# Beside-copies cut into four, and attention work moved between the convolutions, in a four-layer convolution chain

## The reference

```python
# layer 0
q2 = _l2n(q2 / (jnp.sum(q2, axis=2, keepdims=True) + 1e-07), axis=2)
k2 = _l2n(k2 / (jnp.sum(k2, axis=2, keepdims=True) + 1e-07), axis=1)
kv = jnp.einsum('bnc,bnd->bcd', k2, v)
t2 = jnp.einsum('bnc,bcd->bnd', q2, kv) / math.sqrt(N)
attn = (v + t2) @ w_ln + b_ln
...
y = jax.nn.leaky_relu(_conv(y, w1, 'VALID') + b1, 0.2)
y = jax.nn.leaky_relu(_conv(y, w2, 'SAME') + b2, 0.2)
y = _conv(y, w3, 'VALID') + b3
return y + shortcut
# layers 1 and 3
y = lax.conv_general_dilated(jax.nn.relu(x), dw_kernel, ..., feature_group_count=C)
y = lax.conv_general_dilated(y + dw_bias, pw_kernel, ...) + pw_bias
```

## Time and profile before

| what | us |
|---|---|
| median of 3 runs (1218.30 to 1224.15) | 1218.42 |
| the profiled execution, its own time | 1220.06 |
| its span on the core | 1218.2 |
| TensorE busy with matmuls (90% of the span) | 1092.2 |
| VectorE busy (70%) | 855.1 |
| ScalarE busy (39%) | 473.6 |
| a full iteration, from one pair convolution's start to the next one's (392.33 to 529.44) | 137.1 |

### The profile page before, as it was taken

One profiled execution on the slowest core, in us unless ns is written; L12 is line 12 of the kernel. 1 busy time (PEld: TensorE's weight loads), 2 busy tenths in 40 slices (PEclk: granted clock), 3 DMA queues, 4 the chain that ended last, 5 costly groups with the idle time before them and its releaser, 6 DMA issues.

```text
span 1218.2 us, 14814 instructions
## 1 busy us (share of the span) xinstructions
PE 1092.2 (90%) x5000; PEld 704.7 (58%) x5000; DVE 855.1 (70%) x1182; ACT 473.6 (39%) x812; POOL 90.4 (7%) x72
## 2 busy tenths in 40 slices
PE   4698779979998999989998999989998999987956
PEld 3465656647664666647664666647664666645414
DVE  6732379955799369965799369965799369962940
ACT  3311534235522644245522644245522644243321
POOL 0300021000200021000200021000200021000000
PEclk9899879989999999999999999999999999998987
DMA  4033513089405943089405943089405930089035
GB/s 61 14 57 46 71 23 39 12 98 120 65 0 71 104 77 39 0 110 117 65 0 72 106 75 39 2 112 113 65 0 76 107 69 1 6 112 125 12 41 73
DMA packets 213503, 72.97 MB, mean 60 GB/s; under 512 B 206464, under 2 KB 207333, under 8 KB 213477
## 3 DMA queue, kind: packets, MB, share of 16 engines
q1 hardware_dynamic: 213476, 72.63, 45.4%
HBM read 10.49 MB, written 6.29 MB: 14 GB/s over the span
## 4 chain that ended last, share of the span: by engine, by line
PE 46%; DVE 23%; issue 16%; DMA 5%; SPq 5%; ACT 4%; DVEq 0%; POOL 0%; ACTq 0%; POOLq 0%
PE bank L1119 12%; DVE dwa L647 8%; DVE dwb L647 5%; PE bank L1095 5%; DMA y_parts<-a_parts 5%; PE bank L1077 4%; PE bank L1122 4%; PE bank L1121 4%; PE bank L1032 3%; SPq L866 3%; PE bank L1187 2%; SPq L862 2%; PE bank L1134 2%; PE bank L1069 2%; PE bank L1042 2%
## 5 line engine op out<-in xcount | busy, mean ns | idle before, releaser
L647 DVE SCALAR_TENSOR_TENSOR dwa<-h1a,dyn,dwa 128x1024 f32<-128x1024 f32 x240 | 293.4, 1273 | 0.0
L1095 PE MATMUL bank<-y_parts,w_h 96*96 96x512 f32 x1152 | 292.9, 403 | 0.0
L1095 PEld LDWEIGHTS bank<-y_parts,w_h 96*96 96x96 f32 x1152 | 184.3, 162 | 104.5 <-issue 21.0
L1119 PE MATMUL bank<-a_parts,wt_h 128*112 128x512 f32 x384 | 122.4, 429 | 60.5 <-DMA y_parts<-a_parts 52.8
L647 DVE SCALAR_TENSOR_TENSOR dwb<-h1b,dyn,dwb 128x1024 f32<-128x1024 f32 x128 | 154.8, 1274 | 0.0
L1095 PE MATMUL bank<-y_parts,w_l 96*96 96x512 f32 x576 | 148.0, 401 | 0.0
L1119 PEld LDWEIGHTS bank<-a_parts,wt_h 128*112 128x112 f32 x384 | 67.1, 185 | 91.2 <-DMA y_parts<-a_parts 34.3
L1095 PEld LDWEIGHTS bank<-y_parts,w_l 96*96 96x96 f32 x576 | 93.4, 162 | 44.3
L967 POOL TENSOR_TENSOR y_parts<-y,y_parts 96x512 fp32r<-96x512 f32 x56 | 67.0, 1199 | 191.9 <-DVE y L686 191.8
L1350 ACT ACTIVATE y<-bank,b2s 96x512 f32<-96x512 f32 x32 | 21.9, 684 | 146.0 <-PE bank L1095 146.0
L961 POOL TENSOR_TENSOR tok<-tok,u 128x1536 f32<-128x1536 f32 x8 | 22.4, 2794 | 727.7 <-DVE u L584 727.7
(11 more groups left out here) (236 smaller groups left out, 1570.6 us busy)
## 6 DMA issues: line engine op xcount, KB each, us to landing
y_parts<-a_parts SPq DMA_DIRECT2D x32, 396.0 KB, 6.1
y_parts<-a_parts SPq DMA_DIRECT2D x64, 192.0 KB, 6.7
tok<-in_x_dram SPq DMA_DIRECT2D x48, 192.0 KB, 4.8
a_parts<-a_parts SPq DMA_DIRECT2D x64, 132.0 KB, 3.8
x_even<-y_parts SPq DMA_DIRECT2D x16, 384.0 KB, 8.0
x_odd<-y_parts SPq DMA_DIRECT2D x16, 384.0 KB, 8.1
out_dram<-dwb SPq DMA_DIRECT2D x32, 192.0 KB, 3.6
y_parts<-a_parts SPq DMA_DIRECT2D x32, 132.0 KB, 4.3
```

Source lines behind the costliest of these rows:

```text
L647: nc.vector.scalar_tensor_tensor(out=dst, in0=tap_input(n, t), scalar=weight, in1=dst, op0=ALU.mult, op1=ALU.add).then_inc(tap_step, 1)
L1095: last = nc.tensor.matmul(bank[0:C2, :], wgt[:, t, :], src[:, rows, cols], start=t + n == 0, stop=t == TAPS - 1 and n == 2)
L1119: nc.tensor.matmul(bank[0:P2, :], wgt[layer][:, kw, :], own[:, rows, kw:kw + W], start=n + kw == 0, stop=False)
```

## The change

Four things are changed together.

- **Copies by quarters.** `copy_beside` takes a quarter (8 pairs of rows) instead of a half, so there are 32 copies for each layer and image instead of 16, each of half the bytes. Quarter m waits for chunks 0 to m+1 of the high and low parts, and for layer 1 to `conv2` chunk m+1, for layer 3 to `l1` chunk m. `pair_conv` waits at every chunk for its own quarter.
- **Scores earlier.** TensorE does l1 0, transposes 0 and 1, l1 1, transposes 2 and 3, scores, and then project 2 and 3, then l1 2 and 3.
- **Attention between layer 3's chunks.** After l1 come l3 0, routing, sums, l3 1, tokens 0, gather, l3 2, tokens 1, attention weights, l3 3, tokens 2, halo, tokens 3, conv1.
- **ScalarE and VectorE follow.** ScalarE squares the first four scores before it takes l1 1 out, the other four after it, then finishes units 4 and 5, and then does project's chunks 2 and 3 and the fourth powers. VectorE begins the norms before it writes x2's low parts 2 and 3; `sums_out` is split, and its first part (`sums_apart`) stands ahead of `mix_weights`.

```diff
@@ -245,7 +245,7 @@
             sem(n) for n in ("xq_ready", "y1_slope", "y1_max", "y1h_ready", "y1l_ready", "y1l_last"))
         y2_slope, y2_ready, v_ready, ah1_ready, al1_ready = (sem(n) for n in ("y2_slope", "y2_ready", "v_ready", "ah1_ready", "al1_ready"))
 
-        b_copied = {n: (sem(f"b{n}_first_copied"), sem(f"b{n}_rest_copied")) for n in (L1, L3)}
+        b_copied = {n: [sem(f"b{n}_copied{m}") for m in range(PCHUNKS)] for n in (L1, L3)}
         x2_ready, x2h_ready, x2l_ready, x2_copied = (sem(n) for n in ("x2_ready", "x2h_ready", "x2l_ready", "x2_copied"))
         mean_ready, rwz_ready, rw_ready = (sem(n) for n in ("mean_ready", "rwz_ready", "rw_ready"))
         tap1_ready = sem("tap1_ready")
@@ -600,13 +600,16 @@
                 nc.vector.tensor_tensor(q, q, columns(r[:, :, :], 0, [[1, 2 * RUN], [0, C]]), ALU.mult).then_inc(q_scaled, 1)
                 attn2_chain.end()
 
-            def sums_out(image):
+            def sums_apart(image):
 
                 bank = ring_a.bank(A_G)
                 dve.wait_ge(g_done, 2 * image + 2)
                 for at in (0, ODD_AT):
                     nc.vector.tensor_copy(gs[at:at + C, :], bank[at:at + C, 0:SUMS]).then_inc(gs_ready, 1)
-                both_parities = bank[0:SUMS, 128:128 + C]
+
+            def sums_out(image):
+
+                both_parities = ring_a.bank(A_G)[0:SUMS, 128:128 + C]
                 dve.wait_ge(gt_done, image + 1)
                 nc.vector.tensor_copy(gt[:, :], both_parities).then_inc(gt_ready, 1)
                 nc.vector.tensor_tensor(gm[:, :], both_parities, gram_mask[:, :], ALU.mult).then_inc(gt_ready, 1)
@@ -796,16 +799,18 @@
                 if back is not None:
                     l3_low_part(back, 2)
                     l3_low_part(back, 3)
+                if attn is not None:
+                    norms_begin(attn)
                 x2_low_part(f, 2)
                 mean_out(f)
                 x2_low_part(f, 3)
                 route(f)
                 if attn is not None:
-                    norms_begin(attn)
+                    sums_apart(attn)
                 mix_weights(f)
                 if attn is not None:
+                    sums_out(attn)
                     norms_end(attn)
-                    sums_out(attn)
                     conv1_weights(attn)
                 conv1_out(attn, f)
                 if attn is None:
@@ -815,6 +820,7 @@
             prepare_conv2()
             norms_begin(0)
             norms_end(0)
+            sums_apart(0)
             sums_out(0)
             conv1_weights(0)
             conv1_out(0, None)
@@ -847,8 +853,8 @@
                     dst = columns(tok[j * W:(j + 1) * W, :, :, :], at, [[TOK, RUN], [1, C]])
                     sp.dma_start(dst, src[of, j]).then_inc(x_loaded, 16)
 
-        def copy_beside(sp, n, half):
-            r0, rows = half * PAIRS // 2, PAIRS // 2
+        def copy_beside(sp, n, m):
+            r0, rows = m * ROWS, ROWS
             rest = C - 2 * SPARE
             below, above = slice(r0 + 2, r0 + rows + 2), slice(r0, r0 + rows)
             here, behind = slice(r0, r0 + rows), slice(r0 + 1, r0 + rows + 1)
@@ -859,11 +865,11 @@
                             (dst[0:rest, :, here, :], own[2 * SPARE:C, :, below, :]),
                             (dst[rest:APART, :, here, :], own[ODD_AT:P2, :, above, :])):
                 to, frm = (t.rearrange("p a h w -> p a (h w)") for t in (to, frm))
-                sp.dma_start(to, frm).then_inc(b_copied[n][half], 16)
+                sp.dma_start(to, frm).then_inc(b_copied[n][m], 16)
             for part in range(2):
                 for to, frm in ((dst[APART:APART + rest, part, here, 1:W + 1], own[2 * SPARE:C, part, below, 0:W]),
                                 (dst[APART + rest:128, part, here, 1:W + 1], own[ODD_AT:P2, part, above, 0:W])):
-                    sp.dma_start(to, frm).then_inc(b_copied[n][half], 16)
+                    sp.dma_start(to, frm).then_inc(b_copied[n][m], 16)
 
         def copy_x2(sp, f):
 
@@ -885,20 +891,20 @@
 
         def beside_l1(sp, f):
 
-            for half in range(2):
-                chunks = 3 + half
+            for m in range(PCHUNKS):
+                chunks = min(m + 2, PCHUNKS)
                 wait(sp, ah1_ready, PCHUNKS * f + chunks)
                 wait(sp, al1_ready, PCHUNKS * f + chunks)
-                wait(sp, conv2_done, CHUNKS * f + 3 + 2 * half)
-                copy_beside(sp, L1, half)
+                wait(sp, conv2_done, CHUNKS * f + m + 2)
+                copy_beside(sp, L1, m)
 
         def beside_l3(sp, b, l1_images):
-            for half in range(2):
-                wait(sp, l1_done, PCHUNKS * l1_images - 2 + 2 * half)
-                chunks = 3 + half
+            for m in range(PCHUNKS):
+                wait(sp, l1_done, PCHUNKS * l1_images - 3 + m)
+                chunks = min(m + 2, PCHUNKS)
                 wait(sp, ah3_ready, PCHUNKS * b + chunks)
                 wait(sp, al3_ready, PCHUNKS * b + chunks)
-                copy_beside(sp, L3, half)
+                copy_beside(sp, L3, m)
 
         @block.sync
         def _(sp):
@@ -1110,8 +1116,7 @@
 
                 for m in chunks:
                     bank = ring.take(pe, image, places[m])
-                    if m % 2 == 0:
-                        pe.wait_ge(b_copied[layer][m // 2], 16 * B_COPIES * (image + 1))
+                    pe.wait_ge(b_copied[layer][m], 16 * B_COPIES * (image + 1))
                     rows = slice(m * ROWS, (m + 1) * ROWS)
                     for n, (wgt, part) in enumerate(((wt_h, 0), (wt_l, 0), (wt_h, 1))):
                         own, beside = a_parts[layer][:, part, 1:PAIRS + 1, :], b_parts[:, part, :, :]
@@ -1226,29 +1231,36 @@
                         rows, cols = slice(0, (M1, M2)[n]), slice(n * M1, (M1, M)[n])
                         nc.tensor.matmul(banks[7][0:C2, 192 + cols.start:192 + cols.stop], ones[rows, 0:C2], norm1[rows, cols],
                                          start=True, stop=True).then_inc(prep_pe, 1)
-                l1(f, (0, 1))
-                if back is not None:
-                    project(back, (2, 3))
-                if attn is not None:
-                    transpose_x(attn, (0, 1))
-                l1(f, (2,))
-                if attn is not None:
-                    transpose_x(attn, (2, 3))
-                l1(f, (3,))
+                for m in range(2):
+                    l1(f, (m,))
+                    if attn is not None:
+                        transpose_x(attn, (2 * m, 2 * m + 1))
                 if attn is not None:
                     attention_scores(attn)
+                if back is not None:
+                    project(back, (2, 3))
+                l1(f, (2, 3))
+                if back is not None:
+                    l3(back, (0,))
                 routing(f)
-                if back is not None:
-                    l3_and_out(back)
                 if attn is not None:
                     attention_sums(attn)
                 if back is not None:
-                    out_tokens(back, (PCHUNKS - 1,))
+                    l3(back, (1,))
+                    out_tokens(back, (0,))
                 if attn is not None:
                     attention_gather(attn)
-                expand_halo(f)
+                if back is not None:
+                    l3(back, (2,))
+                    out_tokens(back, (1,))
                 if attn is not None:
                     attention_weights(attn)
+                if back is not None:
+                    l3(back, (3,))
+                    out_tokens(back, (2,))
+                expand_halo(f)
+                if back is not None:
+                    out_tokens(back, (PCHUNKS - 1,))
                 conv1(attn, f)
 
             transpose_x(0, range(4))
@@ -1282,9 +1294,9 @@
                     nc.scalar.activation(xcm[0:P2, n * BANK:(n + 1) * BANK], ring_a.bank(A_XT + n)[0:P2, :], ACT.Copy)\
                         .then_inc(xcm_ready, 1)
 
-            def scores_out(image):
-
-                for n in range(8):
+            def scores_out(image, groups):
+
+                for n in groups:
                     act.wait_ge(qk_done, 8 * image + n + 1)
                     src = ring_a.bank(A_QK + n)[:, 0:4 * C2].rearrange("p (m b s c) -> p m b s c", m=2, b=2, s=2)
                     for s, at in enumerate((Q_AT, K_AT)):
@@ -1428,35 +1440,35 @@
                 l1_high_part(f, PCHUNKS - 1)
                 if back is not None:
                     project_affine(back, f + 1, 1)
+                if attn is not None:
+                    x_out(attn, (0, 1))
                 l1_out(f, (0,))
+                if attn is not None:
+                    x_out(attn, (2, 3))
+                    scores_out(attn, range(0, 4))
+                l1_out(f, (1,))
+                if attn is not None:
+                    scores_out(attn, range(4, 8))
                 if back is not None:
                     finish_unit(back, 4)
```

(26 more changed lines are left out.)

6 lines of the change are left out of this document (3 added, 3 removed).

## The result

| | before | after |
|---|---|---|
| median of the runs shown with the result, us | 1219.41 (1218.30 to 1227.47, 6 runs) | 1231.84 (1229.58 to 1232.97, 6 runs) |
| the profiled execution, us | 1220.06 | 1231.61 |
| its span, us | 1218.2 | 1229.8 |
| its mean granted TensorE clock | 0.960 | 0.951 |

The ratio of the two is 1.0086, with a 95% interval from 1.0056 to 1.0116. The forecast was 1206.5, its range 1189 to 1221. The result lies above the range, and on the other side of no change; with 0.5% as the bound it is "slower", to which the prediction gave 0.12.

A forecast was written before the change was run, and what follows sets the result against it. TensorE was taken as the bound, waiting mainly for the beside-copies. Gains of 1.8 (six iterations), 0.8 (iteration 0), 1.3 (iteration 7) and 8.3 us (last image), 12.2 from 1220.06, gave 1207.9; the runs' lower median made it 1206.5, range 1189 to 1221.

The forecast's parts named there:

- wait for unit 4: Before project 2: a new TensorE wait of 1.9 us, since ScalarE finishes unit 4 only behind the squares.
- one quarter's issues: SyncE's queue: eight issues for a quarter take 5.3 us, between 4.7 us by bytes and 7.8 us.
- idle before it: At the halo: TensorE waits 3.3 us for the x2 copies, a new idle stretch in each full iteration.
- the chain: Squares, unit 4, project 2, layer 3's quarters 1 to 3, then x2 in SyncE's queue; x2 lands at 441.5.
- The last image: Layer 3 of the last image: quarters let l3 3 start 8.3 us earlier, bounds 5 and 9.
- the start: Iteration 0: x2 lands earlier for the halo, 0.8 us gained, bounds -1 and 2.
- the clock: Behind the halo's idle stretch: half clock costs about 1.1 us an iteration, bounds 0 and 2.0.
- In proportion: Rule for the half clock's cost at the halo: scaled from 2.0 us behind 4.59 us idle to 3.3 us idle.
- the point of decision: 5.7 us a quarter, at which x2 lands as late as TensorE came to the halo before.
- Iteration 7: Iteration 7: x2's copies are issued earlier and the halo follows, 1.3 us gained, bounds -3 and 4.
- the second: Rival: 5.6 us a quarter and full clock cost lose 1.8 us an iteration; 1216 us, chance 0.26 with the third.
- The fourth: Rival: the queue becomes the bound at 6.5 us a quarter; 1248 us, chance 0.11.

The follow-up runs named there:

- quarters alone: Kernel before with its old order of work, only the beside-copies cut into quarters; 1204.01 us, ratio 0.9865.
- both waits filled: Changed kernel with unread matmuls, 7 ahead of the wait for unit 4 and 17 ahead of the wait for x2; 1209.80 us, ratio 0.9911.
- only the halo's wait filled: Changed kernel with 17 unread matmuls ahead of the wait for x2 only; 1216.08 us, ratio 0.9957.
- x_even by ScalarE: Changed kernel with the two x_even copies issued from ScalarE's queue behind routing, x_odd left on SyncE's; 1220.57 us, ratio 0.9998.
- scores early only: Changed kernel with attention's sums, gather, weights and norms back behind layer 3, the scores left early; 1237.46 us, ratio 1.0140.
- the order alone, with halves: Changed kernel with its new order of work, the beside-copies by halves again; 1281.97 us, ratio 1.0498.
- unit 4 first: Changed kernel with ScalarE finishing unit 4 before the last four squares instead of behind them; 1229.79 us, ratio 1.0066.
- first half quartered: Kernel before with only layer 1's first half cut into two quarters, all other copies halves; 1208.91 us, ratio 0.9909.
- transposes early: Kernel before with quarters, the four transposes moved up between l1 0, l1 1 and project 2, two picks ahead of its wait; 1193.27 us, ratio 0.9784.
- mixed: Same order as transposes early, but quarters only for layer 1's first half and the last image's layer 3; 1188.27 us, ratio 0.9741.
- sums in the gap: The mixed kernel with attention's sums moved ahead of layer 3's chunk 2; 1177.42 us, ratio 0.9653.

## Why the prediction was wrong, point by point

Relative to l1 0's start (388.92 in iteration 2, about 529.6 in iteration 3):

| step | forecast | iteration 2 | iteration 3 |
|---|---|---|---|
| scores start | 9.2 | 9.4 | 9.4 |
| pause inside the scores (0.76 before) | not changed | 0.94 | 0.94 |
| wait for unit 4 | 1.9 | 1.59 | 1.59 |
| project 2 starts | 17.9 | 18.2 | 18.2 |
| layer 3's quarter 1 issued | 22.7 | 25.2 | 23.0 |
| one quarter's issues | 5.3 | 5.57 | 5.55 |
| x2 issued | 38.6 | 41.9 | 39.6 |
| from there to the halo | 15.2 | 16.2 | 15.8 |
| halo | 53.8 | 58.1 | 55.4 |
| idle before it | 3.3 | 4.46 | 4.82 |

**Right.** l1 0 starts behind project 1 without a wait. The queue, not TensorE, sets the halo, in all six full iterations. The wait for unit 4 stands where it was put, with 1.59 us; the 0.94 us inside the scores are the pause that the forecast counted with the 6.75 us of the scores (0.76 before). Iteration 3, where project 2 runs at full clock, follows the chain to 1.6 us in 53.8. The last image gained 8.1 us where 8.3 was forecast, the start 1.0 where it was 0.8. The experiments bear the mechanism out as well: without the reordering x2 is in time (quarters alone), and the attention work between layer 3's chunks does no harm (without it, 5.6 us more).

**The step that failed: the clock.** The term was 1.1 us an iteration for the wait at the halo, and nothing for the one at project 2. The runs with the waits filled put the clock at 3.8 us in all, about 2 behind the halo and the rest at project 2. The error has three parts.

- *The sum.* "In proportion" to the 2.0 us behind 4.59 us of the earlier trace rows, 3.3 us of idleness would have cost 1.4 us and not 1.1; by its own rule the prediction had no gain left in the loop.
- *The scale.* The price is not in proportion to the idle time: 4.46 us were followed by 3.4 us at 1.2 GHz and 4.82 by 6.8.
- *The term left out.* The wait of 1.9 us before project 2 was costed by its own length, without a reason. The trace of before has one short wait in each full iteration, 0.76 us in the scores with the clock kept, and one of about 4.5 us with the clock lost; between the two the price was unknown and should have had bounds.

```profile
417.59 1.57 PE L1032 MATMUL bank<-qkw,xcm 113*128 113x192 f32 x8 [0.76 <-ACT tok L1292]
```

In iteration 2 these two waits, 0.94 and 1.59 us, were followed by 6.8 us at 1.2 GHz, in iteration 3, with the same lengths, by none. On top of its direct cost the slow project 2 delays low part 2, and with it the chain to x2: 25.2 in place of 22.7.

**Sizes.** A quarter took 5.55 to 5.57 us, just under the 5.7 that I gave as the point of decision, and x2 landed 15.8 to 16.2 us after its issue, not 15.2. Over three quarters that is 0.8 us, with x2 1.4 to 1.8. The kernel with both waits filled shows the like: it gains 0.3 us an iteration, where the forecast without its clock term was 1.4. So of the 3.8 us an iteration between the forecast (0.3 gained) and the periods (3.5 lost), 2.7 are the clock and 1.1 the chain. By the table of the Trainium skill's page "DMA: Bandwidth & Descriptors", section Bandwidth, a quarter was estimated at 6.6 us; the row is well below that.

**Iteration 7** was 2.2 us longer, where I had 1.3 shorter; bounds of -3 and 4 on the gain did hold it. It is the same step: the halo came when it came before, behind 9.33 us of waiting, and the expansion behind it ran at 1.2 GHz. The prediction had no clock term there.

**Slips without effect.** "l1 0 and l1 1 taking 5.6 us to 397.95" is l1 0 alone (l1 1 starts there); the 2.0 us are right. The end of the squares was put at 404.6, where its own terms give 404.4.

**In sums**: 23.7 us lie between forecast (-12.2) and result (+11.5): 20.2 in the six iterations, 3.5 in iteration 7. Of the rivals the second, everything in the loop is given back and a little more, named the right place and direction; it had 1.8 us lost in each iteration and was short too, by the clock at project 2. The fourth had the right sign and the right place, the queue as the bound, but for the wrong reason: it needed 6.5 us a quarter.

**What stays open** is why waits of the same length are followed by half clock in one iteration and not in another. For the waits ahead of project 2 the profiled executions show, in the six full iterations:

| waits, us | kernel | followed by a stretch at 1.2 GHz |
|---|---|---|
| 0.94 and 1.6 | after; only the halo's wait filled | 4 and 6 of 6 |
| 0.94 and 1.6 | x_even by ScalarE; scores early only | 5 and 5 of 6 |
| 0.94 and 1.6 | the order alone, with halves | 0 of 6 |
| 1.89 | unit 4 first | 5 of 6 |
| 3.0 | quarters alone; first half quartered | 3 and 4 of 6 |
| 0.8 | transposes early; mixed; sums in the gap | 0, 0 and 0 of 6 |

From 1.6 us up the length doesn't decide it, nor whether it is one wait or two. The stretches here begin during the wait or within 2 us behind it. What the runs do show is that filling both waits removes it in all six iterations.

## What to carry to other kernels

Before work is moved ahead of something, follow what that something releases, through the queues to the last transfer: here 7 us of scores ahead of a projection were no more than moved work on TensorE, and x2 was issued 41.9 us after l1 0's start in place of 31.4. Cost each new wait of TensorE with the half clock that may follow it, as a range with both ends: here the waits of 0.8 us before project 2 were never followed by it, those of 1.6 us and more were in some iterations and not in others. Cut a transfer only where its reader waits for the first part; where it doesn't, the whole one leaves the queue free for the next.

## What the runs showed of the hardware

- Waits of 0.94 and 1.59 us, 1.6 us apart, can be followed by 6.8 us at 1.2 GHz, a single one of 1.89 by 3.4 us, and the same waits by none. Filling waits with unread matmuls raised the mean clock from 0.951 to 0.977 and took 22 us off 1231.8.
- DMAs within a core, issued by SyncE: eight for a quarter (0.67 MB) take 5.55 us, 0.61 to 0.7 us each, and are not held back; in that stretch the DMA share is 0.60 and the rate 112 GB/s, against 143 GB/s for halves:

```profile
414.00:431.00 17.00, 17.00 (x126) 12.37 (x123) 11.20 (x21) 9.47 (x14) 2.81 (x1) 1.00 0.60 112
```

- A second queue moved no more, 122 GB/s against 121: a quarter's issues went from 5.5 to 11.6 us while x_even's two copies ran beside them.
- x2's four copies of 384 KB took 15.6 to 16.2 us from first issue to TensorE's first matmul behind quarters. Behind halves the DMA engines were idle by 15.5 us after the first issue. So it did not make them shorter that quarters stood ahead of them.
